# The last cross-attention: memory projected per head pair with the weights stationary

## What is computed

```python
xn = (x - mu) * jax.lax.rsqrt(var + EPS) * ln_g + ln_b      # b, 100, 512
q = _split_heads(xn @ Wq)                                    # 16 heads of 64
kv = xn @ Wkv
k = _split_heads(kv[..., :INNER])
v = _split_heads(kv[..., INNER:])
mem = _split_heads(memories @ Wm)                            # memories: b, 722, 512
k = jnp.concatenate([k, mem], axis=2)                        # 822 keys
v = jnp.concatenate([v, mem], axis=2)
dots = jnp.einsum('bhid,bhjd->bhij', q, k) * scale
attn = jax.nn.softmax(dots, axis=-1)
out = jnp.einsum('bhij,bhjd->bhid', attn, v)
return out.transpose(0, 2, 1, 3).reshape(b, n, h * d) @ Wo + bo
```

## Time and profile before

| | |
|---|---|
| median of 3 runs | 1912.72 us (1911.47 to 1913.72) |
| the profiled execution's own time | 1913.55 us |
| its span, first to last instruction | 1911.9 us |
| PE busy in the span | 1673.1 us (88%) |
| DVE, ACT, POOL busy | 1078.0, 776.3, 136.2 us |
| mean granted clock of TensorE | 0.934 |
| the touched stage | about 805 to 1503 us of the span |

### The profile page before, as it was taken

The page is one execution under the profiler, slowest core; times in us unless marked ns, Lnnn a source line. Parts: engine busy times, 40 slices in busy tenths (PEclk is TensorE's granted clock), DMA queues, the critical chain, the costliest instruction groups (busy, mean ns, idle before and its releaser), DMA issues. The chain is left out here.

```text
span 1911.9 us, 31342 instructions
## 1 busy us (share of the span) xinstructions
PE 1673.1 (88%) x11296; PEld 1354.9 (71%) x11296; DVE 1078.0 (56%) x1840; ACT 776.3 (41%) x1400; POOL 136.2 (7%) x177
## 2 busy tenths in 40 slices
PE   5996359999999689899999999999998719999993
PEld 5775359999999389567676766767665519999981
DVE  5775547667767543135554545555465326766765
ACT  2453135555555132134443434444354115445440
POOL 4000310000000301100000000000000040000004
PEclk9998579999999889899999999999999659999997
DMA  9300265565566344231111111111100065655634
GB/s 339 137 9 1 80 227 204 204 213 197 200 209 227 84 149 147 79 103 29 38 28 39 29 32 41 28 38 28 27 14 6 1 216 177 216 211 191 216 138 123
DMA packets 98510, 223.45 MB, mean 117 GB/s; under 512 B 36696, under 2 KB 57304, under 8 KB 83324
## 3 DMA queue, kind: packets, MB, share of 16 engines
q1 hardware_dynamic: 82988, 175.72, 28.1%
q0 software_dynamic: 15440, 46.56, 7.0%
HBM read 180.61 MB, written 41.62 MB: 116 GB/s over the span
## 5 line engine op out<-in xcount | busy, mean ns | idle before, releaser
L955 DVE TENSOR_TENSOR e_lo<-e_raw,e_hi 128x2048 fp32r<-128x2048 f32 x118 | 270.2, 2290 | 128.7 <-ACT e_hi L1018 128.7
L918 PE MATMUL banks<-e_xh,e_hi 128*128 128x256 f32 x1024 | 292.5, 286 | 12.3 <-DVE e_xl L971 7.5
L918 PE MATMUL banks<-e_xl,e_hi 128*128 128x256 f32 x1024 | 291.8, 285 | 0.0
L918 PE MATMUL banks<-e_xh,e_lo 128*128 128x256 f32 x1024 | 291.7, 285 | 0.0
L1593 PE MATMUL banks<-a_wm,a_ch 128*128 128x512 f32 (+1 forms) x768 | 248.0, 404 | 22.3 <-DVE a_v L1721 11.3
L1018 ACT CAST e_hi<-e_raw 128x2048 fp32r<-128x2048 f32 x118 | 224.7, 1904 | 70.2 <-PE banks L935 28.6
L918 PEld LDWEIGHTS banks<-e_xh,e_hi 128*128 128x128 f32 x1024 | 197.9, 193 | 20.8 <-issue 8.3
L918 PEld LDWEIGHTS banks<-e_xl,e_hi 128*128 128x128 f32 x1024 | 197.9, 193 | 5.5
L918 PEld LDWEIGHTS banks<-e_xh,e_lo 128*128 128x128 f32 x1024 | 197.9, 193 | 0.0
L1593 PEld LDWEIGHTS banks<-a_wm,a_ch 128*128 128x128 f32 (+1 forms) x768 | 134.0, 183 | 61.8 <-issue 15.6
L1767 DVE COPY a_PT<-banks 128x200 f32<-128x200 f32 x128 | 46.5, 363 | 189.0 <-PE banks L1638 188.8
(11 more groups left out here) (234 smaller groups left out, 2674.6 us busy)
## 6 DMA issues: line engine op xcount, KB each, us to landing
e_raw<-wout SPq DMA_DIRECT2D x50, 1024.0 KB, 4.9
e_raw<-w SPq DMA_DIRECT2D x34, 1024.0 KB, 4.9
e_raw<-wgate SPq DMA_DIRECT2D x17, 1024.0 KB
e_raw<-wup SPq DMA_DIRECT2D x17, 1024.0 KB, 4.8
a_craw<-ctxT SPq DMA_DIRECT2D x40, 256.0 KB, 2.9
e_xs<-slot_rows SPq DMA_DIRECT2D x18, 512.0 KB
slot_outs<-e_y POOLq DMA_DIRECT2D x16, 512.0 KB, 3.2
slot_rows<-a_zero POOLq DMA_DIRECT2D x15, 512.0 KB, 10.3
```

Of the source, the lines that this page charges most:

```text
L918: mm = nc.tensor.matmul(ps[:, bank, 0:CAP], w[:, cc, cut], x[:, cc, :], start=t == 0, stop=t == len(terms) - 1)
L955: nc.vector.tensor_tensor(lo[g % 2][i][:], raw[q % RAW][:], hi[g % 2][i][:].bitcast(F32), ALU.subtract)\
```

## The change

The job changes sides. `memory` holds a 128x128 piece of Wm stationary (the 128 output channels of one head pair) and moves the context's tokens, 362 or 360 columns, so two half jobs of twelve matmuls give the keys of one pair directly, channels on the partitions. ACT copies the first half to `a_kT`, DVE the second. `turn_values` transposes six blocks of `a_kT` into values, copied by ACT. There are 16 half jobs a batch where there were 12 jobs. Every step is the same: it makes the keys of pair p+2 and the values of pair p+1; only the last two steps of all have no half jobs. The context is held whole for two batches (`a_ch`, `a_cl`), and is split by 128 rows of its width (cc), in steps m = 1 to 4 of the batch ahead. Own values are loaded for each pair. `attended` now takes the pair just before. The two heads' turned probabilities are copied by ACT (first head) and DVE (second).

```diff
-    MIDDLE = {0: 0, 1: 2, 2: 3, 3: 5, 4: 7, 5: 9, 6: 10, 7: 11}
-    END = {0: 1, 2: 4, 3: 6, 4: 8}
-    SPLIT = {0: (1, 2), 1: (1, 3), 2: (1, 4), 3: (1, 5), 6: (2, 0), 7: (2, 1)}
+    HALF = [(0, 362), (362, S - 362)]
+    OUTPUT_AT = 1
+    SPLIT_AT = {1 + cc: cc for cc in range(DC)}
...
     # SP
+                def context(b, cc):
+                    after(sp, cl_done, DC * (b - 1) + cc + 1)
+                    sp.dma_start(craw[cc][:], a["ctxT"][bass.ds(b, 1), 128 * cc:128 * cc + 128, :]
+                                 .rearrange("b p s -> p (b s)")).then_inc(craw_in[cc], 16)
+                def own(b, m):
...
+                    after(sp, sc, p - SLOTS + 1)
                     sp.dma_start(q[s][:], ...)
                     sp.dma_start(kT[s][:, 0:T], ...)
+                    after(sp, yd, p - SLOTS + 1)
+                    sp.dma_start(v[s][0:T, 0, :], s1.v[bass.ds(b, 1), :, 128 * m:128 * m + 128]
+                                 .rearrange("b t n -> t (b n)")).then_inc(v_in[s], 16)
...
+                def step(b, u, m):
+                    own(b, m + SLOTS - 1)
+                    if m in SPLIT_AT and later(b):
+                        context(b + 1, SPLIT_AT[m])
...
     # TensorE
+                    for cc in range(DC):
...
+                        for t, (w, x) in enumerate(((s1.wm[0], ch[u]), (s1.wm[0], cl[u]), (s1.wm[1], ch[u]))):
+                            mm = nc.tensor.matmul(ps[:, 6 + half, 0:wide], w[:, cc, cut], x[:, cc, start:start + wide],
+                                                  start=cc == 0 and t == 0, stop=cc == DC - 1 and t == 2)
...
+                def step(b, u, m):
+                    p = IC * b + m
+                    scores(p, b, m)
+                    prev = exists(p - 1)
+                    if prev:
+                        turn(p - 1, back(b, m)[1], 0)
+                    memory_ahead(b, u, m, 0)
+                    if prev:
+                        turn(p - 1, back(b, m)[1], 1)
...
+                    memory_ahead(b, u, m, 1)
+                    if exists(p + 1):
+                        turn_values(p + 1, (m + 1) % IC)
+                    if prev:
+                        attended(p - 1, *back(b, m))
+                    if m == OUTPUT_AT and exists(p - IC):
+                        output(b - 1, 1 - u)
...
     # DVE
+                    highest(p, m, 0)
+                    highest(p, m, 1)
+                    normalise(p, m, 0)
+                    if exists(p - 1):
+                        turned(p - 1, (m - 1) % IC)
+                    normalise(p, m, 1)
+                    if exists(p + 2):
+                        keys(p + 2, (m + 2) % IC)
+                    if m in SPLIT_AT and later(b):
+                        split(b + 1, 1 - u, SPLIT_AT[m])
...
     # ACT
+                def split(b, u, cc):
+                    act.wait_ge(craw_in[cc], 16 * b + 16)
+                    nc.scalar.copy(ch[u][:, cc, :], craw[cc][:]).then_inc(ch_done, 1)
```

More of the change, by code:

```diff
@@ L1512, in over_steps, with batch, later @@
         def over_steps(eng, step):
[L1515 to L1522, removed]
+            def batch(b, u):
+                for m in range(IC):
+                    step(b, u, m)
+            batch(0, 0)
             with eng.Fori(0, (B - 2) // 2) as i:
[L1524 to L1527, removed]
+                batch(2 * i + 1, 1)
+                batch(2 * i + 2, 0)
+            batch(B - 1, 1)
         def exists(p):
-            return type(p) is not int or 0 <= p < B * IC
+            return type(p) is not int or 0 <= p < PAIRS
+        def later(b):
+            return type(b) is not int or b < B - 1
         with nc.Block() as block:
@@ L1585, in _ @@
             def _(pe):
[L1586 to L1596, removed]
@@ L1714, in _ @@
+                for half in range(2):
+                    memory(0, 0, 0, 0, half)
+                for half in range(2):
+                    memory(1, 0, 0, 1, half)
+                turn_values(0, 0)
                 pe.wait_ge(o_in, 32)
                 over_steps(pe, step)
-            def copy_values(eng, copy, done, b, u, n, bank):
-                nb, g = ORDER[n]
-                size = MB[nb][1]
-                eng.wait_ge(val, NV * b + n + 1)
-                copy(v[u][0:size, 1 + nb, 512 * g:512 * g + 512], ps[0:size, bank, :]).then_inc(done, 1)
@@ L1723, in begin @@
-            def begin(split, evacuate):
-                for nb in range(3):
-                    split(0, nb)
-                for n in range(NV):
-                    evacuate(0, 0, n, n % 4)
-                    if n in FINAL and FINAL.index(n) + 3 < NB + 2:
-                        split(0, FINAL.index(n) + 3)
+                for two in range(2):
+                    turn(PAIRS - 1, IC - 1, two)
+                attended(PAIRS - 1, B - 1, IC - 1)
+                output(B - 1, 1)
             @block.vector
@@ L1801, in _ @@
+                for cc in range(DC):
+                    split(0, 0, cc)
+                for m in range(2):
+                    keys(m, m)
                 over_steps(dve, step)
+                turned(PAIRS - 1, IC - 1)
+                add_output(B - 1)
             @block.scalar
             def _(act):
-                act.sem_inc(ys, 2)
-                def split(b, nb):
-                    b, nb = b + nb // NB, nb % NB
-                    size = MB[nb][1]
-                    act.wait_ge(craw_in[nb % 3], 32 * b + 16 * (nb // 3) + 16)
-                    pb, pn_ = (b, nb - 3) if nb >= 3 else (b - 1, nb + 3)
-                    after(act, val, NV * pb + FINAL[pn_] + 1)
-                    nc.scalar.copy(ch[nb % 3][:, :, 0:size], craw[nb % 3][:, :, 0:size]).then_inc(ch_done, 1)
@@ L1839, in step @@
[L1839 removed]
+                    nc.scalar.copy(yT[u][:, m, :], ps[:, 6, 384:384 + T]).then_inc(ys, 1)
+                def step(b, u, m):
                     p = IC * b + m
[L1841 to L1860 removed]
@@ L1862, in _ @@
-                begin(split, evacuate)
-                keys(0, 0)
+                    if exists(p - 1):
+                        turned(p - 1, (m - 1) % IC)
+                    exponent(p, m, 0)
+                    exponent(p, m, 1)
+                    if exists(p + 2):
+                        keys(p + 2, (m + 2) % IC)
+                    if exists(p + 1):
+                        values(p + 1, (m + 1) % IC)
+                    if exists(p - 1):
+                        attended(p - 1, u if m >= 1 else 1 - u, (m - 1) % IC)
@@ L1864, in _ @@
+                    if m in SPLIT_AT and later(b):
+                        split(b + 1, 1 - u, SPLIT_AT[m])
+                for cc in range(DC):
+                    split(0, 0, cc)
+                for m in range(2):
+                    keys(m, m)
+                values(0, 0)
                 over_steps(act, step)
+                turned(PAIRS - 1, IC - 1)
+                attended(PAIRS - 1, 1, IC - 1)
 def build(nc, a):
```

325 lines of the change are left out of this document (118 added, 207 removed).

## The result

The changed kernel takes **1944.58 us** (median of 4, 1943.76 to 1946.77), the kernel before, run beside it, 1912.10 (1910.17 to 1913.72). The ratio is 1.0172, with a 95% interval of 1.0154 to 1.0190: slower by 1.7%, 32 us. The prediction was 1933 us, slower, with a range of 1905 to 1960.

A forecast was written before the change was run, and what follows sets the result against it. The prediction took TensorE's instruction stream, with a few per cent of waits, to bound the last attention stage. It summed -32 us of work and +51 us of exposed context loads to +19 on 1913.55: about 1933 us, range 1905 to 1960.

The forecast's parts named there:

- the new stage without its waits: Last attention stage without any wait: 665.4 us against 697.6, a gain of 32 us.
- loads asked for too late: Context loads issued only in the step that wants them: 2.3 us lost, 22 times, 51 us.
- The mechanism: Late context load delays ACT's cast, then DVE's work, then TensorE's turn of the values; step ends at 11.5, not 9.2.
- 1.56 + 0.70 + 2.05 + 0.70 + 2.05 + 0.77 + 1.35 = 9.18 us: One new TensorE step: scores, turn, half job, turn, half job, value transposes, attended values.
- The start of the stage: Last attention's start to first scores: 17.5 us where it was 39, as steps wait for Wo; part only moved work.
- the seven full batches hardly change: Last attention's full batches: 16 half jobs, 32.8 us, stand where 12 jobs, 34.4 us, stood.
- Batches 1 to 6, 482.2: TensorE time of six full batches in the last attention, without waits, each eight steps plus output, 80.4 us.
- Rival 1: Context loads cost little, as short as 2.0 us or hidden; kernel faster, 1881 us if nothing waits; chance 0.17.
- Rival 2: No change, 1914 us: a 2.0 us load, or cheaper 362-column matmuls (153 ns) offsetting the stall; chance 0.08.
- Rival 3: TensorE's clock falls behind gaps in the stalled steps, costing 22 x 1.6 = 36 us: 1969 us; chance 0.11.

The follow-up runs named there:

- e3: Changed kernel with the context load issued a step earlier and the loop's back edge moved behind the output product; 1865.67 us, ratio 0.9754 to the kernel before.
- e1: Changed kernel with one order swapped on SP: context load ahead of the own loads, so asked for a step earlier; 1882.99 us, ratio 0.9845.
- e2: Changed kernel with its loop turned by two steps, closing behind the output product of m = 1, loads still late; 1922.63 us, ratio 1.0057.
- e8: Kernel with early context and edge behind the output, its output product cut to one of eight matmul groups; 1820.36 us, only steps read.
- e6: Changed kernel, context loads cut to 100 of 722 columns (50 KB) from the second batch; stage 680.0 us against 703.6, whole time says nothing.
- e7: Changed kernel with the context loaded a step earlier and the loop turned by five steps, closing between m = 4 and 5; 1875.50 us, ratio 0.9806.
- e5: Kernel before with its loop turned to close between m = 7 and 0, one back edge left; 1915.25 us against 1912.24, ratio 1.0018.

## Why the prediction was right, point by point

The parts of the change can be laid side by side, since each of them had the kernel before run beside it (medians of 1912.1 to 1913.3 us):

| term | predicted | measured | from |
|---|---|---|---|
| the new stage without its waits | -32 | -47 | e3 less before |
| loads asked for too late | +51 | +62 (57 with the edge moved) | after less e1 (e2 less e3) |
| the loop's back edge | 0 | +17 (22 with the late loads) | e1 less e3 (after less e2) |
| sum | +19 | +32 | |

**The mechanism** is the predicted one: e1 shows it by the order of two calls on SP, and the chain in the stalled step is the one written down, piece by piece: context asked for at 0.80 (predicted 0.8), cast at 4.04 (3.7), maximum at 5.69 (5.4), normalisation at 8.01 (7.7), the turn of the values at 9.66 (9.4), end at 11.79 (11.5). Every piece behind the landing is 0.3 us late, which is the landing: 3.2 us and not 2.9 in the list of DMA issues.

```profile
a_craw<-ctxT SPq DMA_DIRECT2D x32, 361.0 KB, 3.2
```

The size was too small because each of the 22 stalls is counted from a plain step, and that is 8.94 us, not 9.18: 11.5 less 8.94 plus 0.3 is 2.9, times 22 is 63.

The rule in the Trainium skill, page "DMA: Bandwidth & Descriptors", section "Rules for kernel authors", to issue a DMA early and wait late, was on the right side: in e1 the same load is asked for 8.4 us before its use and costs nothing.

**The first mis-sized term**, "1.56 + 0.70 + 2.05 + 0.70 + 2.05 + 0.77 + 1.35 = 9.18 us". TensorE's timeline of a plain step, in the last batch:

```profile
1495.49 1.63 PE L1596 MATMUL banks<-a_kT,a_q 64*100 64x512 f32 x8
1497.05 0.81 PE L1607 MATMUL banks<-ident,a_P 100*100 100x100 f32 x7
1497.63 0.41 PE L1562 MATMUL banks<-a_ch,a_wm 128*128 128x362 f32 x1
1497.88 0.33 PE L1562 MATMUL banks<-a_cl,a_wm 128*128 128x362 f32 x1
...
1499.54 0.33 PE L1562 MATMUL banks<-a_ch,a_wm 128*128 128x362 f32 x1
1499.70 0.76 PE L1607 MATMUL banks<-ident,a_P 100*100 100x100 f32 x7
1500.25 0.41 PE L1562 MATMUL banks<-a_ch,a_wm 128*128 128x360 f32 x1
...
1502.31 0.82 PE L1583 MATMUL banks<-ident,a_kT 128*128 128x128 f32 x6
1503.06 1.43 PE L1623 MATMUL banks<-a_PT,a_v 100*64 100x100 f32 x28
1504.41 1.11 PE L1596 MATMUL banks<-a_kT,a_q 64*100 64x512 f32 x4
```

From start to start: scores 1.56, turn 0.58, half job 2.07, turn 0.55, half job 2.06, turn of the values 0.75, attended 1.35; 8.92 in all. The half job is right (2.05), and so is its 0.164 a matmul. The turn is not: I took its 0.70 from the earlier trace rows, where the output or a scores product stands behind it, and here a half job does. Its start overlaps the turn's end. That is 0.27 for the two turns of a step. In a row, plain steps are 8.94 us, 0.24 under the predicted 9.18, and 62 of them make 15 us, within 1 us the whole difference between -32 and -47. The start of the stage, 16.3 us from first cast to first scores (17.5), gives 1.

The prediction also says that its 32 us come from the start and the last batch while "the seven full batches hardly change". Its own sum says otherwise: 70.7 + 482.2 is 552.9 us for those batches, 24 under the 576.90 of the earlier trace rows, and the last batch's first six steps and output are 62.0, 13 over the 49.25. In e3 the full batches gain 37 us, the start 23, and the last batch's six steps lose 11 (60.6 us). Of the predicted 24 some 11 are the cheaper jobs (32.8 for 34.4, seven times); the rest is about what TensorE waited in these batches, 15.5 us in the earlier trace rows and nothing in e3.

**The term that was missing** is the edge. "Batches 1 to 6, 482.2" priced every step by its instructions, and the loop moved with the change: the diff replaces a loop that closed behind step m = 1 by one that closes behind m = 7. I read past this. Nothing in the trace of before shows a cost; that 6.9 us of queued output hid it there is inferred from e8, where most of that cover is taken away in the new kernel and a wait appears.

**The rivals.** Rival 1 (a cheap load) is wrong in its premise, the landing is 3.2 us, but its sum is what e1 reaches when the load is moved: it gave 1881 us, and e1 measures 1883, in which 15 us of better steps and 17 us of edges cancel. Its arithmetic for a 50 KB load holds too: it gave a stall of 1.46 us, and most steps of e6 are 1.5 over a plain one. Rival 2 needs 153 ns for 362 columns (the figure that it took from the Trainium skill, page "TensorE: Matmul & The Clock Gate", section "Back-to-back issue gap"); measured, from the second to the twelfth matmul of the half job above, are 1.66 us for ten distances, 166 ns each. The sum did get 15 us better, though by the turns and not by the matmuls. Rival 3 (clock) did not happen where I put it: the granted clock of the stretch with the stalled steps is 1.00.

```profile
1022.72:1075.80 53.08, 45.79 (x402) 37.65 (x400) 26.65 (x48) 23.00 (x53) 0.00 (x0) 1.00 0.14 37
```

Gaps of 1.2 to 1.3 us in a step did not lower the clock; a gap of 7.7 at the edge did, and so did those of 3.8 in e7 and 2.00 in e8 (means of 0.60 and 0.77 over the 7.44 us behind them).

That 1933 lay 12 us from 1944.6 is partly luck: the two errors of +15 and -28 had opposite signs.

## What to carry to other kernels

When a change makes a load step by step instead of ahead, read the order of calls on the issuing queue: here a load that stood behind a wait for the end of the current step was paid in full from its request on, even when it was small (50 KB still cost 1.5 us a time), and the exchange of two lines cured it. When a change moves the place where a hardware loop closes, price it as an edit of its own, and try the longest piece of queued work right ahead of the back edge (17 to 22 us here, for two edges). And take a piece's price from a row in which the same operation stands behind it.

## What the runs showed of the hardware

- A loop's back edge on TensorE's stream costs a wait with no releaser in the profile: 7.73 and 7.71 us (changed kernel, m = 7 to 0), 6.3 twice (e1, the same place), 3.8 and 3.7 (e7, m = 4 to 5), 3.2 (e5), 2.00 twice (e8, 1.0 us of product ahead), nothing that can be seen behind the whole output product of 7 us (before, e2, e3).
- Whether it is the fetch of instructions is not shown, but the rows point there. The list of DMA queues for the 10 us at either edge of the changed kernel, 1075 to 1085 and 1258 to 1268, has three transfers of the instruction queue, where other stretches of that length have none or one (transfers, MB, share; the row is the same at both):

```profile
q8 instruction: 3, 0.05, 2.9%
```

  Seen in windows of 0.25 us, two of the three begin at 1076.00, as TensorE's last matmuls end, and the third at 1080.75, 2.8 us before the scores at 1083.56; at the second edge they start at 1259.75 and 1264.50, with the scores at 1267.24. e1 has one at 1048.00 and one at 1051.25, with the scores at 1054.19. In e7 the last one ahead of the scores starts 3.8 us before them, in e5 3.3, in e8 2.9. So the long waits hold two rounds of transfers, the short ones a single round. Which engine's instructions they carry the profile doesn't say, and no run changed them alone.
- What makes two rounds at one place and one at another, with the same number of steps in the loop, is open. Ahead of both stands the same attended-values product; the address of the loop differs, and I did not try that. It is not the address alone: e1 has TensorE's instructions of the changed kernel, and its wait is 6.3 and not 7.7.
- Behind an edge the granted clock is at its half level, 1.2 GHz, and then full again. At the first edge of the changed kernel a mean of 0.72 over 7.44 us between two levels gives 4.2 us at the half level, where the scores take 3.07 and not 1.63. At other edges the mean of the same length is 0.82 to 0.59 (e7's second, e1's first), so 2.7 to 6.1 us.
